# Head attention in halves of a block: maxima, their transfer and the products per 1024 queries

## The chip, the cores and the metric

The kernel runs on one core of a Trainium2 chip. The metric is the device time of one execution in microseconds (us); the kernel before stands at a median of 3103.95 us. The engines are named as in the profile: PE (matmuls) with PEld (its weight loads), DVE (vector engine), ACT (scalar engine), POOL (GpSimd), and SP, which computes nothing and issues DMAs.

## What is computed

A transformer block with a fast feed-forward layer ahead of it and one behind it. The change is in the attention of the layer between them alone. Its reference, cut to what matters:

```python
q = x @ Wq.T + bq; k = x @ Wk.T + bk; v = x @ Wv.T + bv      # x: 2 x 2048 x 256
qm = q.reshape(d_batch * NB_HEADS, q_len, d_head)            # 32 x 2048 x 16, and km, vm
att = softmax(einsum('nqd,nkd->nqk', qm, km), axis=-1)
...
att_out = einsum('nqk,nkd->nqd', att + batch_pos, vm)        # batch_pos: position bias by head
```

So there are 32 independent blocks (16 heads, 2 batches), each with 2048 queries and 2048 keys of 16 numbers.

## The kernel before

`head_attend` handles the 32 blocks one after another (`BLOCKS` = 32, `n` is the block, `n // 2` the head). A block's 2048 rows are 16 chunks of 128 (`RC` = 16) or four groups of 512 (`QG` = 4). Every engine runs its own program in a fixed order and meets the others by semaphores only. The work of a block:

- **Scans.** `scan(n, e)` on PE, 64 for a block: one chunk of 128 queries against 512 keys, into one of four PSUM banks (`s1_ps`). DVE takes the maximum of two banks at a time (`scan_max`, L1538), 32 for a block. A bank comes free when its maximum is done.
- **Maxima.** `max_parts` on DVE, four small instructions among the first four scan maxima of the next block: the maximum of each query over the four key groups (`nmax`, L1545), its two parts (`mparts`, L1549, L1552), and a transpose in 32 x 32 squares (`mT`, L1558). `load_m` on SP then issues 8 DMAs (L1281) that bring `mT` into two rows of the query stack `qs`, so that the score matmul subtracts the maximum by itself.
- **Scores.** `score(n, c, g)` on PE (L1456), 64 for a block: 128 keys on the partitions against 512 queries, into one of three PSUM turns; ACT takes the exponential into `probs` (L1603), 64 for a block.
- **Products.** `products` on PE (L1467) adds the values times `probs` in one PSUM bank, four matmuls a half, two chunks behind the scores (`LATE` = 2). When the last chunk is in, DVE transposes the bank and takes a reciprocal (`turn_out`, L1565, L1568), and POOL finishes and stores the block (`finish`).
- **Positions.** For each head two `positions` pieces on PE (L1483, 11 matmuls each) once POOL has prepared its sums; ACT copies them out (L1593) and SP stores them (`store_pos`, L1303).

`step(n)` on PE interleaves the scans of later blocks with the scores of block `n`: scan and score alternate, and after each second pair comes a half of products. At its start it waits for the maxima of its block (`m_loaded`). The scans lead by a whole block and 24 (`LEAD` = 6 chunks of 4): before `step(0)` PE has issued 88 scans and both position pieces of head 0, and after the last scan 88 scores are left.

SP's program for block `n`, in this order: wait until the last score of block `n - 1` is made; 12 loads of queries and keys for block `n + 2` (`load_qk`, L902); for even `n` up to 24 five loads for a later head (`load_head`: L1293, L1294, L1295, and two of L1297) and up to 22 one more DMA (`skew`, L1285); two stores of positions (`store_pos`); and last `load_m(n + 1)`. SP issues strictly in that order, and a wait holds everything behind it.

Of the kernel before, what the change touches and what calls it, by code (L numbers as in the profile page):

```python
# [1173 lines left out]
def head_attend(nc, tag, stacks, scan_loaded, ones_set, parts_d, v_d, table_d, skew_d, pos_d, att_d):  # L1174
# [3 lines left out]
    with ExitStack() as ctx:  # L1178
# [14 lines left out]
        UNIT = RC * QG  # L1193
        SCANS = RC * QG
        LEAD, LATE = 6, 2
# [11 lines left out]
        probs = sb("probs", [P, LATE + 1, ROWS])  # L1207
        mx = sb("mx", [P, SLOTS * SCANS])
        nmax = sb("nmax", [P, RC])
        mparts = sb("mparts", [P, PARTS, RC], F32R)  # L1210
        mT = sb("mT", [P, PARTS * RC])
# [32 lines left out]
        MLOADS = QUADS * PARTS  # L1244
# [8 lines left out]
        for n in range(BLOCKS):  # L1253
            for c in range(RC):
                for g in range(QG):
                    turn_of["score", n, QG * c + g] = len(turn_of)
                if c == POS_AT and n // 2 + 1 < HEADS:
                    turn_of["pos", n // 2 + 1, n % 2] = len(turn_of)

        def scores_done(n):  # L1260
            return turn_of["score", n, UNIT - 1] + 1
# [177 lines left out]
        def _(pe):  # L1439
            def scan(n, e):  # L1440
                count = SCANS * n + e
                if e % 2 == 0 and count >= BANKS:
                    pe.wait_ge(s1_free, (count - BANKS) // 2 + 1)
                c, g = e // QG, e % QG
                nc.tensor.matmul(s1_ps[:, e % BANKS, :], qs[0:QKROWS, n % SLOTS, c, :],  # L1445
                                 ks[0:QKROWS, n % SLOTS, g * 4:(g + 1) * 4, :].rearrange("p c t -> p (c t)"),
                                 start=True, stop=True).then_inc(s1_made, 1)
# [6 lines left out]
            def score(n, c, g):  # L1454
                out = take_turn(turn_of["score", n, QG * c + g])
                nc.tensor.matmul(out, ks[LOW:LOW + KR, n % SLOTS, c, :],  # L1456
                                 qs[LOW:LOW + KR, n % SLOTS, g * 4:(g + 1) * 4, :].rearrange("p c t -> p (c t)"),
                                 start=True, stop=True).then_inc(s2_made, 1)

            def products(n, c, half):  # L1460
                if half == 0:
                    pe.wait_ge(s2_free, turn_of["score", n, QG * c + QG - 1] + 1)
                elif c == 0:
                    return
                at, size = (0, 512) if c == 0 else (half * HALF, HALF)
                for g in range(QG):
                    last = nc.tensor.matmul(o_ps[g * COLS:(g + 1) * COLS, at:at + size], vs[:, n % SLOTS, c, :],  # L1467
                                            probs[:, (n + c) % (LATE + 1), g * 512 + at:g * 512 + at + size],
                                            start=(c == 0), stop=(c == RC - 1 and half == 1), tile_position=(0, g * COLS))
                if c == RC - 1 and half == 1:  # L1470
                    last.then_inc(o_made, 1)
# [21 lines left out]
            def step(n):  # L1493
                pe.wait_ge(score_loaded[n % SLOTS], 16 * LOADS * (n // SLOTS + 1))
                pe.wait_ge(m_loaded, 16 * MLOADS * (n + 1))
                pe.wait_ge(v_placed, n + 1)
                for c in range(RC):
                    ahead = n + 1 if c < RC - LEAD else n + 2
                    if c == RC - LEAD and ahead < BLOCKS:
                        pe.wait_ge(scan_loaded[ahead % SLOTS], 16 * LOADS * (ahead // SLOTS + 1))  # L1500
                    for k in range(QG):
                        if ahead < BLOCKS:
                            scan(ahead, (c + LEAD) % RC * QG + k)
                        score(n, c, k)
                        if k % 2 == 0:
                            continue
                        if c >= LATE:
                            if c == LATE and k == 1 and n > 0:
                                pe.wait_ge(turn_step, 2 * n - 1)
                            products(n, c - LATE, k // 2)  # L1510
                        elif n > 0:
                            products(n - 1, RC + c - LATE, k // 2)
                    if c == POS_AT and n // 2 + 1 < HEADS:
                        positions(n // 2 + 1, n % 2)

            pe.wait_ge(constants_set, 4)
            pe.wait_ge(scan_loaded[0], 16 * LOADS)
            for e in range(SCANS // 2):
                scan(0, e)
            for half in range(2):  # L1520
                positions(0, half)
            for e in range(SCANS // 2, SCANS):
                scan(0, e)
            pe.wait_ge(scan_loaded[1], 16 * LOADS)
            for e in range(LEAD * QG):
                scan(1, e)
            for n in range(BLOCKS):
                step(n)
            for c in range(RC - LATE, RC):
                for half in range(2):  # L1530
                    products(BLOCKS - 1, c, half)

        @block.vector
        def _(dve):
            def scan_max(n, e):
                dve.wait_ge(s1_made, SCANS * n + e + 2)
                at = n % SLOTS * SCANS + e
                nc.vector.reduce_max(mx[:, at:at + 2], s1_ps[:, e % BANKS:e % BANKS + 2, :], AX_X).then_inc(s1_free, 1)  # L1538

            def max_parts(m, i):  # L1540

                if i == 0:
                    dve.wait_ge(s1_free, SCANS // 2 * (m + 1))
                    at = m % SLOTS * SCANS
                    nc.vector.reduce_max(nmax[:, :], mx[:, at:at + SCANS].rearrange("p (c g) -> p c g", g=QG),  # L1545
                                         AX_X, negate=True).then_inc(max_step, 1)
                elif i == 1:
                    dve.wait_ge(max_step, MSTEPS * m + 1)
# [471 lines left out]
```

## Time and profile before

| | |
|---|---|
| median of 3 runs | 3103.95 us (3103.12 to 3110.8) |
| profiled execution | 3088.07 us, span 3086.3 us |
| head attention, first scan to last exponential | 826.9 to 2205 us |
| busy over the whole span | PE 92%, DVE 69%, ACT 58%, POOL 29% |
| mean granted PE clock | 0.956 |

Times in the trace count from the span's start. A row of the timeline that merges several instructions (x8) gives the first start and the time until the last end. In brackets stands how long the engine had been idle, and what ended that. An SPq row is a DMA's issue on SP; its landing is later.

### The profile page before, as it was taken

What the parts mean: (1) busy time and instruction counts of PE and PEld (TensorE: products, weight loads), DVE (VectorE), ACT (ScalarE), POOL (GpSimd) and SP (SyncE); (2) the same over time, 40 slices, a digit from 0 to 9 for tenths busy, and PEclk for the clock granted to TensorE, in tenths of its full rate; (3) what the DMA queues carried; (4) which work ended last, traced back from release to release, by engine and by line L of the source; (5) the groups of instructions that cost most, each with busy time, mean ns of one, the idle gap of its engine ahead of it and who ended that gap; (6) DMA issues with size and microseconds to landing.
All of it is one profiled execution on the core that took longest, in us unless ns stands there. A gap on an engine that the chain in (4) does not pass through costs nothing. (4 is left out here: it accounts for less than half of the span.)

```text
span 3086.3 us, 56464 instructions
## 1 busy us (share of the span) xinstructions
PE 2843.5 (92%) x20746; PEld 1731.7 (56%) x20746; DVE 2130.9 (69%) x3331; ACT 1796.6 (58%) x3503; POOL 908.5 (29%) x1482
## 2 busy tenths in 40 slices
PE   5788999998799999999999999999795688899999
PEld 2677888886543333333333333333253377688888
DVE  5445555455589999999999999998053454555544
ACT  3345343334248888888888888888543244444333
POOL 4552310001343333333333333311112554220000
PEclk8999999998779999999999999999897799999999
DMA  8795210105935554444555554442233589221010
GB/s 248 241 298 161 66 40 28 31 25 201 277 49 67 67 67 54 58 60 60 67 67 67 67 64 56 48 48 32 76 105 123 168 284 287 83 63 30 28 31 21
DMA packets 447482, 302.13 MB, mean 98 GB/s; under 512 B 170840, under 2 KB 421820, under 8 KB 447212
## 3 DMA queue, kind: packets, MB, share of 16 engines
q1 hardware_dynamic: 413292, 214.59, 35.4%
q0 software_dynamic: 33920, 83.93, 8.6%
q8 instruction: 170, 2.79, 0.4%
q14 instruction: 100, 0.82, 0.1%
HBM read 183.27 MB, written 118.78 MB: 98 GB/s over the span
## 5 line engine op out<-in xcount | busy, mean ns | idle before, releaser
L1538 DVE TENSOR_REDUCE mx_ha<-s_ps_ha 128x2 f32<-128x1024 f32 x1024 | 1243.5, 1222 | 57.3 <-PE s_ps_ha L1445 49.7
L1603 ACT ACTIVATE probs_ha<-s_ps_ha 128x512 f32<-128x512 f32 x2048 | 1108.8, 595 | 192.7 <-PE s_ps_ha L1456 58.8
L1445 PE MATMUL s_ps_ha<-ks_ha,qs_ha 48*128 48x512 f32 x2048 | 759.3, 454 | 14.0 <-POOL onesr_ha L1411 8.4
L1456 PE MATMUL s_ps_ha<-qs_ha,ks_ha 50*128 50x512 f32 x2048 | 749.6, 446 | 0.8 <-ACT probs_ha L1603 0.2
L1467 PE MATMUL o_ps_ha<-probs_ha,vs_ha 128*32 128x256 f32 (+1 forms) x7936 | 646.7, 398 | 0.9 <-DVE oT_ha L1565 0.9
L1445 PEld LDWEIGHTS s_ps_ha<-ks_ha,qs_ha 48*128 48x128 f32 x2048 | 312.7, 190 | 441.5 <-DVE mx_ha L1538 373.1
L870 ACT ACTIVATE probsT_a<-pT_ps_a 128x512 fp32r<-128x512 f32 x256 | 146.4, 597 | 423.0 <-PE pT_ps_a L744 409.2
L1467 PEld LDWEIGHTS o_ps_ha<-probs_ha,vs_ha 128*32 128x32 f32 x7936 | 156.5, 108 | 359.7 <-issue 186.1
L1456 PEld LDWEIGHTS s_ps_ha<-qs_ha,ks_ha 50*128 50x128 f32 x2048 | 304.9, 185 | 33.0 <-ACT probs_ha L1603 32.6
L699 POOL DMA_INDIRECT rows_a<-ys_d,slots x96 | 90.9, 947 | 627.1 <-PE turn_ps_a L721 576.1
L1395 POOL TENSOR_TENSOR onorm_ha<-oT_ha,rinv_ha 128x256 f32<-128x256 f32 x32 | 19.9, 623 | 837.4 <-DVE rinv_ha L1568 837.4
L787 DVE TENSOR_REDUCE nmax_a<-s_ps_a 128x1 f32<-128x2048 f32 x64 | 146.7, 2292 | 162.2 <-PE s_ps_a L733 161.1
L444 DVE COPY y_p<-y_ps_p 128x256 f32<-128x256 f32 x282 | 119.5, 424 | 188.6 <-PE y_ps_p L574 126.4
L248 POOL DMA_INDIRECT xs_d<-xn_p,row_of_p x192 | 186.6, 972 | 202.3 <-PE xT_ps_p L538 88.6
L476 ACT ACTIVATE h_p<-h_ps_p,wa_p 65x128 f32<-65x128 f32 x282 | 102.7, 364 | 182.8 <-PE h_ps_p L564 141.3
L733 PE MATMUL s_ps_a<-k0T_a,qT_a 128*128 128x512 f32 x768 | 201.0, 406 | 1.9 <-DVE qT_a L801 1.9
L564 PE MATMUL h_ps_p<-xsT_p,wa_p 128*65 128x128 f32 x1128 | 175.3, 278 | 26.2 <-issue 23.4
L733 PE MATMUL s_ps_a<-k1T,qT_a 128*128 128x512 f32 x768 | 190.4, 398 | 0.0
L574 PE MATMUL y_ps_p<-leaf_w_p,h_p 65*128 x564 | 173.8, 390 | 16.5 <-ACT h_p L476 10.2
L766 PE MATMUL o_ps_a<-v_a,probsT_a 128*128 128x512 f32 x512 | 188.8, 408 | 0.0
L766 PE MATMUL o_ps_a<-v,probsT_a 128*128 128x512 f32 x512 | 188.6, 408 | 0.0
L564 PEld LDWEIGHTS h_ps_p<-xsT_p,wa_p 128*65 128x65 f32 x1128 | 133.6, 139 | 75.1 <-issue 45.3
(212 smaller groups left out, 3950.9 us busy)
## 6 DMA issues: line engine op xcount, KB each, us to landing
xs_p<-xs_d SPq DMA_DIRECT2D x282, 128.0 KB
ys_d<-y_p SPq DMA_DIRECT2D x66, 512.0 KB
qs_ha<-parts_d SPq DMA_DIRECT2D x192, 128.0 KB, 6.1
ks_ha<-parts_d SPq DMA_DIRECT2D x192, 128.0 KB, 6.7
parts_d<-parts_hp POOLq DMA_DIRECT2D x32, 512.0 KB, 7.5
xs_d<-y_p SPq DMA_DIRECT2D x6, 1024.0 KB
leaf_w_p<-in_wa SPq DMA_DIRECT2D x4, 1048.0 KB
leaf_w_p<-in_wb SPq DMA_DIRECT2D x4, 1040.0 KB
```

What stands on the lines that cost most here:

```text
L248: pool.indirect_dma_start(xs_d[f], bass.IndirectOffsetOnAxis(row_of[:, f, t:t + 1], 0), xn[:, t, :], None).then_inc(scattered[f], 16)
L564: last = nc.tensor.matmul(h_ps[0:W1C, n % 2, 0:P], wa[:, n % WB, c * W1C:(c + 1) * W1C], xsT[:, n % 2, c, :], start=(c == 0), stop=(c == C ...
L574: nc.tensor.matmul(y_ps[:, n % 2, 0:D], h[:, n % 2], leaf_w[0:W1C, n // SEG % 2, bass.ds(at + LA, D)], start=True, stop=True).then_inc(y_m ...
L733: last = nc.tensor.matmul(s_ps[:, g, :], qT[:, i % 2, hq, c, :], kT[b][:, hk, c, g * 512:(g + 1) * 512], start=(c == 0 and n == 0), stop=( ...
L766: nc.tensor.matmul(o_ps[:, :], probsT[:, 0, g, k * P:(k + 1) * P], value.rearrange("p h d -> p (h d)"), start=first, stop=False)
L787: nc.vector.reduce_max(nmax[:, :], s_ps[:, :, :].rearrange("p a b -> p (a b)"), AX_X, negate=True).then_inc(max_done, 1)
L870: nc.scalar.activation(probsT[:, 0, g, :], pT_ps[:, g % 2, :], ACT.Identity).then_inc(pT_high, 1)
L1445: nc.tensor.matmul(s1_ps[:, e % BANKS, :], qs[0:QKROWS, n % SLOTS, c, :], ks[0:QKROWS, n % SLOTS, g * 4:(g + 1) * 4, :].rearrange("p c t - ...
L1456: nc.tensor.matmul(out, ks[LOW:LOW + KR, n % SLOTS, c, :], qs[LOW:LOW + KR, n % SLOTS, g * 4:(g + 1) * 4, :].rearrange("p c t -> p (c t)") ...
L1467: last = nc.tensor.matmul(o_ps[g * COLS:(g + 1) * COLS, at:at + size], vs[:, n % SLOTS, c, :], probs[:, (n + c) % (LATE + 1), g * 512 + at ...
L1538: nc.vector.reduce_max(mx[:, at:at + 2], s1_ps[:, e % BANKS:e % BANKS + 2, :], AX_X).then_inc(s1_free, 1)
L1603: nc.scalar.activation(probs[:, (n + c) % (LATE + 1), g * 512:(g + 1) * 512], s2_ps[:, turn % TURNS, :], ACT.Exp).then_inc(s2_free, 1)
```

## The change

A block becomes two units `u` (`UNITS` = 64), each with half of its queries, that is 1024 of them: chunks 0, 1, 4, 5, 8, 9, 12, 13 for the even unit, and the others for the odd one (`chunk_of`). A unit has 32 scans, 32 scores and 32 exponentials of the same sizes as before, and 16 chunks of products with four matmuls each. Everything that was done once a block with the maxima is done once a unit: the four small DVE instructions on 8 columns where there were 16, and `load_m`, which now has 16 DMAs of 4 rows where there were 8 of 16 rows. `mT` has two buffers. `LEAD` = 12 chunks of 2 is again 24 scans, but now beyond a unit: 56 scans come ahead of the first score, and 56 scores behind the last scan. The two position pieces of head 0 stand behind 40 and 48 scans, where both stood behind 32. The wait for the constants comes behind the first 32 scans.

The core of the diff:

```diff
-        UNIT = RC * QG
-        SCANS = RC * QG
-        LEAD, LATE = 6, 2
+        UNITS = 2 * BLOCKS
+        UC = RC // 2
+        PAIR = 2
+        UNIT = RC * PAIR
+        SCANS = UC * QG
+        RING = 2 * SLOTS
+        LEAD, LATE = 12, 2
...
-        MLOADS = QUADS * PARTS
+        MLOADS = QUADS * PARTS * 2
...
+        def chunk_of(u, e):
+
+            k = e // QG
+            return k % QUADS * QUADS + u % 2 * 2 + k // QUADS
...
-            def load_m(n):
-                sp.wait_ge(mT_made, n + 1)
+            def load_m(u):
+                k = u // 2 % SLOTS
+                sp.wait_ge(mT_made, u + 1)
                 for i in range(QUADS):
                     for part in range(PARTS):
                         row = LOW + QKROWS + part
-                        at = i * COLS + part * RC
-                        sp.dma_start(qs[row:row + 1, n % SLOTS, :, i * COLS:(i + 1) * COLS].bitcast(F32),
-                                     mT[at:at + RC, :]).then_inc(m_loaded, 16)
+                        for b in range(2):
+                            at = i * COLS + part * UC + b * QUADS
+                            chunks = qs[row:row + 1, k, u % 2 * 2 + b::QUADS, i * COLS:(i + 1) * COLS]
+                            sp.dma_start(chunks.bitcast(F32), mT[at:at + QUADS, u % 2, :]).then_inc(m_loaded, 16)
...
+            load_m(0)
             for half in range(2):
                 store_pos(0, half)
-            load_m(0)
             for n in range(BLOCKS):
...
                 if n // 2 + 1 < HEADS:
                     store_pos(n // 2 + 1, n % 2)
+                load_m(2 * n + 1)
                 if n + 1 < BLOCKS:
-                    load_m(n + 1)
+                    load_m(2 * n + 2)
...
-            def step(n):
-                pe.wait_ge(score_loaded[n % SLOTS], 16 * LOADS * (n // SLOTS + 1))
-                pe.wait_ge(m_loaded, 16 * MLOADS * (n + 1))
-                pe.wait_ge(v_placed, n + 1)
+            def step(u):
+                n = u // 2
+                if u % 2 == 0:
+                    pe.wait_ge(score_loaded[n % SLOTS], 16 * LOADS * (n // SLOTS + 1))
+                    pe.wait_ge(v_placed, n + 1)
+                pe.wait_ge(m_loaded, 16 * MLOADS * (u + 1))
...
+            for u in range(UNITS):
                 for e in range(0, SCANS, 2):
-                    scan_max(n, e)
-                    if n > 0 and e // 2 <= MSTEPS:
-                        max_parts(n - 1, e // 2)
+                    scan_max(u, e)
+                    if u > 0 and e // 2 <= MSTEPS:
+                        max_parts(u - 1, e // 2)
```

On SP, the program of one block with head loads (`n` = 0), behind the 12 loads of `load_qk`; `mT_made` is the semaphore of the transpose, `s2_free` that of the copied positions, `s2_made` that of the scores. Before:

```order
L1293 DMA band_ha<-skew_d 128x384
L1294 DMA far_ha<-skew_d 128x128
L1295 DMA far_ha<-skew_d 128x128
L1297 DMA vp_ha<-vh_d 128x16x16 x2
...
L1303 DMA pos_d<-pos_ha 128x8x16 [waits s2_free_ha]
L1303 DMA pos_d<-pos_ha 128x8x16
L1281 DMA qs_ha<-mT_ha 1x16x32 [waits mT_made_ha]
L1281 DMA qs_ha<-mT_ha 1x16x32 x7
L902 DMA qs_ha<-parts_d 16x16x128 [waits s2_made_ha]
```

The same place after the change:

```order
L1305 DMA band_ha<-skew_d 128x384
L1306 DMA far_ha<-skew_d 128x128
L1307 DMA far_ha<-skew_d 128x128
L1309 DMA vp_ha<-vh_d 128x16x16 x2
...
L1315 DMA pos_d<-pos_ha 128x8x16 [waits s2_free_ha]
L1315 DMA pos_d<-pos_ha 128x8x16
L1294 DMA qs_ha<-mT_ha 1x4x32 [waits mT_made_ha]
L1294 DMA qs_ha<-mT_ha 1x4x32 x15
L1294 DMA qs_ha<-mT_ha 1x4x32 [waits mT_made_ha]
L1294 DMA qs_ha<-mT_ha 1x4x32 x15
L902 DMA qs_ha<-parts_d 16x16x128 [waits s2_made_ha]
```

Behind the same loads and stores now stand 32 DMAs in two batches with a wait each: the first is for the second half of the block under way, the second for the first half of the next block.

On DVE, the maxima of the first block and what follows them, before:

```order
L1538 TENSOR_REDUCE mx_ha<-s_ps_ha 128x2 [waits s1_made_ha] x33
L1545 TENSOR_REDUCE nmax_ha<-mx_ha 128x16 [waits s1_free_ha]
...
L1558 STREAM_TRANSPOSE mT_ha<-mparts_ha 128x32 [waits max_step_ha]
L1538 TENSOR_REDUCE mx_ha<-s_ps_ha 128x2 [waits s1_made_ha] x29
L1545 TENSOR_REDUCE nmax_ha<-mx_ha 128x16 [waits s1_free_ha]
```

The same after the change:

```order
L1547 TENSOR_REDUCE mx_ha<-s_ps_ha 128x2 [waits s1_made_ha] x17
L1554 TENSOR_REDUCE nmax_ha<-mx_ha 128x8 [waits s1_free_ha]
...
L1567 STREAM_TRANSPOSE mT_ha<-mparts_ha 128x32 [waits max_step_ha]
L1547 TENSOR_REDUCE mx_ha<-s_ps_ha 128x2 [waits s1_made_ha] x13
L1554 TENSOR_REDUCE nmax_ha<-mx_ha 128x8 [waits s1_free_ha]
```

The first maxima come after 17 large reduces, where it was after 33, and from one transpose to the next unit's first small reduce stand 13 large ones where there were 29.

## Rows read from the trace of the kernel before

**Rows 1.** The page's costliest groups, for the head attention's DVE and ACT.

```profile
L1538 DVE TENSOR_REDUCE mx_ha<-s_ps_ha 128x2 f32<-128x1024 f32 x1024 | 1243.5, 1222 | 57.3 <-PE s_ps_ha L1445 49.7
L1603 ACT ACTIVATE probs_ha<-s_ps_ha 128x512 f32<-128x512 f32 x2048 | 1108.8, 595 | 192.7 <-PE s_ps_ha L1456 58.8
```

**Rows 2.** Windows in mid-attention: window, length, PE, PEld, DVE, ACT, POOL, clock, DMA.

```profile
1300.00:1600.00 300.00, 299.85 (x2816) 117.30 (x2818) 290.09 (x277) 254.66 (x474) 108.74 (x233) 1.00 0.54 66
```

**Rows 3.** Timeline of SP, a block with head loads and the next.

```profile
1466.28 0.33 SPq L902 DMA_DIRECT2D qs_ha<-parts_d  x1
...
1475.90 6.53 SPq L1297 DMA_DIRECT2D vp_ha<-vh_d  x2
...
1484.90 1.22 SPq L1303 DMA_DIRECT2D pos_d<-pos_ha  x2
1498.87 4.94 SPq L1281 DMA_DIRECT2D qs_ha<-mT_ha  x8
1507.39 0.33 SPq L902 DMA_DIRECT2D qs_ha<-parts_d  x1
...
1514.76 3.25 SPq L1303 DMA_DIRECT2D pos_d<-pos_ha  x2
```

**Rows 4.** Timeline of all engines where a step starts.

```profile
1499.97 13.56 DVE L1538 TENSOR_REDUCE mx_ha<-s_ps_ha 128x2 f32<-128x1024 f32 x11
...
1507.83 0.18 PEld L1445 LDWEIGHTS s_ps_ha<-ks_ha,qs_ha 48*128 48x128 f32 x1 [0.41 <-issue]
...
1508.17 0.39 PE L1445 MATMUL s_ps_ha<-ks_ha,qs_ha 48*128 48x512 f32 x1
```

**Rows 5.** Instructions on `mT`, `mparts` and `nmax`: ns min/median/max, first and last start.

```profile
L1281 SPq DMA_DIRECT2D qs_ha<-mT_ha x256: 502/589/1864, 881.0 to 2156.3; - x128
L1558 DVE STREAM_TRANSPOSE mT_ha<-mparts_ha x32: 194/200/211, 880.8 to 2151.7; 128x32 f32<-128x32 f32 x32
...
DMA to landing us min/median/max: 1.6/1.7/3.4
...
L1549 DVE CAST mparts_ha<-nmax_ha x32: 161/162/185, 877.6 to 2151.2; 128x16 fp32r<-128x16 f32 x32
L1552 DVE TENSOR_TENSOR mparts_ha<-nmax_ha,mparts_ha x32: 164/166/805, 878.9 to 2151.4; 128x16 fp32r<-128x16 f32 x32
...
L1545 DVE TENSOR_REDUCE nmax_ha<-mx_ha x32: 207/207/220, 876.4 to 2151.0; 128x16 f32<-128x64 f32 x32
```

**Rows 6.** Timeline of the head attention's first stretch.

```profile
826.92 2.07 PE L1445 MATMUL s_ps_ha<-ks_ha,qs_ha 48*128 48x512 f32 x4 [8.35 <-POOL onesr_ha L1411]
...
849.26 2.07 SPq L1297 DMA_DIRECT2D vp_ha<-vh_d  x2
...
850.59 2.29 PE L1483 MATMUL s_ps_ha<-vpp_ha,bandp_ha 128*128 128x256 f32 x9 [3.58 <-POOL distantp_ha L1356]
...
855.44 10.81 DVE L1538 TENSOR_REDUCE mx_ha<-s_ps_ha 128x2 f32<-128x1024 f32 x9 [7.17 <-PE s_ps_ha L1445]
...
889.81 0.79 PE L1456 MATMUL s_ps_ha<-qs_ha,ks_ha 50*128 50x512 f32 x1
```

**Rows 7.** The last scan in the timeline, and the exponentials of all blocks.

```profile
2149.30 0.39 PE L1445 MATMUL s_ps_ha<-ks_ha,qs_ha 48*128 48x512 f32 x1
...
L1603 ACT ACTIVATE probs_ha<-s_ps_ha x2048: 589/597/617, 890.6 to 2204.4; 128x512 f32<-128x512 f32 x187
```

**Rows 8.** Timeline of SP: a DMA of 128 rows (`wo`) and one of 3 rows (`bo`).

```profile
2221.63 0.42 SPq L1682 DMA_DIRECT2D wo_hc<-in_wo  x1
2222.10 0.35 SPq L1682 DMA_DIRECT2D bo_hc<-in_bo  x1
```

**Rows 9.** Windows, as in Rows 2, behind stretches in which PE did little.

```profile
890.00:900.00 10.00, 9.91 (x45) 5.66 (x46) 7.10 (x6) 5.99 (x12) 2.45 (x5) 0.61 1.23 121
...
2655.00:2660.00 5.00, 1.19 (x7) 1.19 (x8) 2.06 (x3) 2.65 (x4) 0.58 (x1) 0.92 0.09 26
2660.00:2665.00 5.00, 4.51 (x17) 3.31 (x15) 4.53 (x12) 4.74 (x15) 0.96 (x1) 0.74 0.02 3
```

More of the change, by code:

```diff
@@ L1452, in take_turn, with score, products @@
                 return s2_ps[:, turn % TURNS, :]
[L1454 to L1457, printed above, removed]
-                                 start=True, stop=True).then_inc(s2_made, 1)
[L1460 to L1470, printed above, removed]
+            def score(u, c, g):
+                out = take_turn(turn_of["score", u, PAIR * c + g])
+                k, first = u // 2 % SLOTS, u % 2 * 2
+                queries = qs[LOW:LOW + KR, k].rearrange("p (j c) t -> p j (c t)", c=QUADS)[
+                    :, 2 * g:2 * g + 2, first * P:(first + 2) * P]
+                nc.tensor.matmul(out.rearrange("p (j t) -> p j t", j=2), ks[LOW:LOW + KR, k, c, :], queries,
+                                 start=True, stop=True).then_inc(s2_made, 1)
+            def products(u, c):
+                pe.wait_ge(s2_free, turn_of["score", u, PAIR * c + PAIR - 1] + 1)
+                at = u % 2 * HALF
+                for i in range(QUADS):
+                    last = nc.tensor.matmul(o_ps[i * COLS:(i + 1) * COLS, at:at + HALF], vs[:, u // 2 % SLOTS, c, :],
+                                            probs[:, (RC * u + c) % (LATE + 1), i, :],
+                                            start=(c == 0), stop=(c == RC - 1), tile_position=(0, i * COLS))
+                if c == RC - 1 and u % 2 == 1:
                     last.then_inc(o_made, 1)
@@ L1491, in positions @@
                 add(onesr[:, :], distantp[:, k, 1], 0, stop=True).then_inc(s2_made, 1)
-            def step(n):
-                pe.wait_ge(score_loaded[n % SLOTS], 16 * LOADS * (n // SLOTS + 1))
-                pe.wait_ge(m_loaded, 16 * MLOADS * (n + 1))
-                pe.wait_ge(v_placed, n + 1)
-                for c in range(RC):
[L1498 to L1513, printed above, removed]
@@ new lines, in step @@
+            def step(u):
[4 more added lines that the diff above has]
+                pe.wait_ge(m_loaded, 16 * MLOADS * (u + 1))
+                for c in range(RC):
+                    ahead = PAIR * (c + LEAD)
+                    to, e = u + 1 + ahead // SCANS, ahead % SCANS
+                    if to % 2 == 0 and e == 0 and to < UNITS:
+                        pe.wait_ge(scan_loaded[to // 2 % SLOTS], 16 * LOADS * (to // 2 // SLOTS + 1))
+                    for k in range(PAIR):
+                        if to < UNITS:
+                            scan(to, e + k)
+                        score(u, c, k)
+                    if c >= LATE:
+                        if c == LATE and u % 2 == 0 and n > 0:
+                            pe.wait_ge(turn_step, 2 * n - 1)
+                        products(u, c - LATE)
+                    elif u > 0:
+                        products(u - 1, RC + c - LATE)
+                    if c == POS_AT and u % 2 == 0 and n // 2 + 1 < HEADS:
@@ L1514, in step @@
                         positions(n // 2 + 1, n % 2)
+            pe.wait_ge(scan_loaded[0], 16 * LOADS)
+            for e in range(SCANS):
+                scan(0, e)
             pe.wait_ge(constants_set, 4)
[L1517 to L1524, printed above, removed]
@@ L1525, in _ @@
-            for e in range(LEAD * QG):
+            for e in range(LEAD * PAIR):
+                if e % 8 == 0 and e > 0:
+                    positions(0, e // 8 - 1)
                 scan(1, e)
-            for n in range(BLOCKS):
-                step(n)
+            for u in range(UNITS):
+                step(u)
             for c in range(RC - LATE, RC):
-                for half in range(2):
-                    products(BLOCKS - 1, c, half)
+                products(UNITS - 1, c)
         @block.vector
```

92 lines of the change are left out of this document (48 added, 44 removed).

## The prediction

> **What bounds the kernel now.** I read the page's costliest groups first. DVE's large maximum and ACT's exponential are the two big groups of the head attention: 1024 of 1222 ns and 2048 of 595 ns [rows 1]. Then a window in its middle: DVE works 290.1 of 300 us, ACT 254.7, and PE is shown busy throughout, at a granted clock of 1.00 [rows 2]. A busy PE says little here, so I looked at the timeline where a step starts: eleven maxima follow each other in 13.56 us, 1.233 us each, while PE's next scan had stood idle 0.41 us [rows 4]. So PE waits for DVE, and the attention runs at DVE's pace: a block takes 1507.39 - 1466.28 = 41.11 us from one last score to the next [rows 3], of which 32 large maxima are 39.5 and the four small instructions 0.735 (207, 162, 166 and 200 ns) [rows 5].
>
> The third view is the queue of SP, which the change loads. After a block's last score SP issues loads and stores for 1486.12 - 1466.28 = 19.84 us in a block with head loads, and until 1518.01, that is 10.6 us, in one without [rows 3]. Then it sits until the maxima are transposed. From the first issue of `load_m` (1498.87) to PE's first scan in the new step (1507.83) there are 8.96 us [rows 3, 4]. The eight DMAs need 7 x 0.6175 us (4.94 / 8) and 1.7 us to land, 6.0 us [rows 3, 5]. So 3.0 us are spare, and nobody waits for the maxima today.
>
> **What the change removes.** Two things at the ends. (1) Behind the last scan (2149.3) the exponentials go on until 2205 [rows 7]: 88 scores at some 0.62 us. 56 are left afterwards, so 32 x 0.62 = 19.9 us fewer, where DVE stays the bound. (2) Ahead of the first position piece PE waits 3.58 us for POOL, and DVE then has been idle 7.17 us [rows 6]. Eight scans later POOL's sums (850.6) are just there; two idle spells of some 1 us remain, a gain of 5 us. That the first score comes at some 863 instead of 889.8 [rows 6] gives nothing by itself, as DVE has the same 1024 maxima to do.
>
> **What it adds on DVE.** The small instructions come 64 times, not 32. On half the columns they are nearly as long, since their shortest kin of 16 columns take 162 ns and the transpose keeps its shape [rows 5]. I take 0.70 us a unit (bounds 0.37, half of now, and 0.735), so 2 x 0.70 - 0.735 = 0.66 us more a block, 21 us in all. By (1), (2) and this the time would hardly move: -4 us.
>
> **What it adds on SP decides.** `load_m` has 16 DMAs for each unit. Its window does not grow: from a unit's transpose to the scan that opens the next step there are the same seven maxima, 8.96 us. The issue of a 4-row DMA is not in the trace. Upper bound: as now, 0.6175 us with the gap. Lower bound: the 3-row DMA at 0.35 us, 0.38 with the gap [rows 8]. That one reads from memory, while a 128-row neighbour of it takes 0.42, so few rows save 0.07 to 0.11 us of it; taken from 0.589 [rows 5], with the gap, this gives 0.51, my value. The last lands 15 x 0.51 + 1.7 = 9.35 us after the first issue, 9.45 with an allowance of 0.1 for waking PE. That is 0.5 us beyond the window.
>
> A page puts the landing otherwise: the Trainium skill, "DMA: Bandwidth & Descriptors", section "Anatomy of one DMA", gives a DMA a fixed cost of about 2.0 us, which doesn't shrink with its size. The trace shows 1.7 us for this very transfer [rows 5]; by the page's figure each unit would wait 0.3 us longer, an estimate of 19 us over 62 units. I go by the trace.
>
> Once the wait is in the loop, the unit's time is a cycle. From the scan that opens the step: 0.73 us until DVE has its two banks (1507.83 to 1508.56) [rows 4], 8 maxima of 1.233, small ones of 0.70, makes 11.3 us to the next transpose; then 9.45. That is 20.75 us for an odd unit. The even one also has the block's turn-out and positions: 41.11 - 39.46 - 0.735 = 0.9 us now, and I take 1.2, since DVE's slack to hide them is used up. A block without head loads: 2 x 20.75 + 1.2 = 42.7 us.
>
> In the 13 blocks with head loads (n = 0, 2, ..., 24) the order on SP costs more. `load_m(2n + 1)` stands behind 19.84 us of loads and stores, and these start with the last score of the unit before. The maxima are ready some 13 us after it and wait for the queue. They are in at 19.84 + 9.45 = 29.3 us; the even unit's step began at 0.8 (20.75 less 19.9 us of scores), so it lasts 28.5 us, and the block 28.5 + 20.75 = 49.25. Behind the waiting PE stand scans, scores and products alike, so DVE and ACT stop too. The long piece of SP's list is the two `vp` loads, 6.53 us [rows 3]; they are unchanged.
>
> Sum. The first step starts at 863: SP is free at 851.3, the first unit's maxima are transposed at some 853.5 (20 maxima of 1.233 behind 826.9, with 1.2 us for the first scans and 0.70), then 9.45 [rows 6]. 13 x 49.25 + 18 x 42.7 = 1409, with 1 more for block 0, whose four position stores now come behind its `load_m`: the last block starts at 2273. Its two units take 19.9 and 19.5 us of scores: the end is at 2312, against 2205, so **+107 us**; both ends' gains are in this.
>
> To that comes the clock. Behind a stretch in which PE did 1.19 us of work in 5, the granted clock is 0.74 over the next 5 us, about 2.6 us at the 1.2 GHz level; behind the opening scans it is 0.61 over 10 us, 7.8 us at that level [rows 9]. PE's work in 1.233 us is 0.83 (0.41 idle) [rows 4], 1.66 at half the clock: a quarter of that time is lost, 0.7 to 2.0 us. With a stop of some 7 us in each of 13 blocks: 9 to 26 us, I take 18. Together +125 us. The profiled execution has 3088.07 us, so 3213 there; it lies 16 us under the median of the runs, whose 3103.95 gives **3229 us**.
>
> **The rivals.**
> - *A 4-row DMA costs as much as one of 16 rows.* For it: that all eight take the same time [rows 3, 5]. Then 15 x 0.6175 + 1.8 = 11.06 us, a unit 22.36, a plain block 45.9, one with head loads 19.84 + 11.06 - 2.46 + 22.36 = 50.8. Sum 1487 from 864.5 on: +187, with the clock +205: 3309 us.
> - *It costs 0.38.* For it: the 3-row row [rows 8]; against: it is another kind of transfer. Then 7.5 us, inside the window. Plain blocks run at DVE's pace, 41.11 + 0.66 = 41.8; those with head loads take 19.84 + 7.5 - 0.4 + 20.4 = 47.3. Sum 1367 from 861 on: +64, with the clock +82: 3186 us.
> - *The clock falls at every unit.* PE stops at each step for the maxima. A gap of 0.41 us at each pair leaves 1.00 now [rows 2, 4], and mine of 0.8 is not much longer, which speaks against it. It would cost 0.7 to 2.0 us for 51 more units, +69: 3298 us. The Trainium skill, "TensorE: Matmul & The Clock Gate", section "HAM oscillation — how this bites in real kernels", describes this: PE stops for a DMA at every tile and starts each one throttled.
> - *The queue is through in time: not slower.* The price hangs on the `vp` pair: 6.53 us behind the loads, but 2.07 us when the queue is empty [rows 3, 6]. From the point at which SP is free some 13.4 us after the last score (20.9 - 7.5), with DMAs of 0.38, nothing waits. Then -4 us: 3100 us. Against it: the loads ahead of the pair stay. If the small instructions fell into DVE's idle 9.9 us in 300 [rows 2] as well: -25, 3079 us.
>
> **How the numbers follow.** Chances: my forecast 0.52 (its own range 3200 to 3265), full price 0.19, low price 0.15, clock at every unit 0.07, in time 0.05, and faster 0.02. The range runs from under the low price with no clock loss (3104 + 64 = 3168) to the full price with 26 us of it (3104 + 187 + 26 = 3317) and a little over: 3165 to 3325. It leaves the last two cases out, and some of the tails. Within 0.3% (9 us) is about what a measurement can't tell from no change. Faster 0.02, same 0.05, slower 0.93.
>
> **What the profile after would show.** Right: the issue of `qs_ha<-mT_ha` at some 0.48 us, x1024; in 13 blocks an SP timeline where these issues follow the position stores without a pause, and there a DVE wait for scans of 6 to 8 us; DVE busy for 0.84 of a block with head loads and 0.97 of a plain one; the first score near 863; the last exponential near 2312. Wrong: maxima at 97% in all blocks, an issue of 0.59 or 0.35, or `vp` loads of 2 us. The largest single doubt is the issue time of the small DMA: 0.1 us of it is worth 35 us downwards and 75 us upwards.

## The result and the profile after

| | before | after |
|---|---|---|
| median of 4 runs | 3104.83 us | 3546.56 us (3528.43 to 3568.62) |
| ratio | | 1.1424, 95% interval 1.1382 to 1.1467 |
| profiled execution | 3088.07 us | 3529.82 us, span 3528.0 us |
| head attention, first scan to last exponential | 1378 us | 835.3 to 2641.0, 1806 us |
| mean granted PE clock | 0.956 | 0.867 |

The change costs 442 us, not 125. Of it 428 lie in the head attention; the first scan also comes 8 us later, and that start varies between 810.5 and 835.3 in the profiles below without regard to the edits.

The costliest groups of the page after, in the place of [rows 1]; at the end of a row stands the idle time ahead of the group:

```profile
L1547 DVE TENSOR_REDUCE mx_ha<-s_ps_ha 128x2 f32<-128x1024 f32 x1024 | 1241.6, 1220 | 475.3 <-PE s_ps_ha L1458 472.0
L1614 ACT ACTIVATE probs_ha<-s_ps_ha 128x512 f32<-128x512 f32 x2048 | 1112.0, 595 | 586.9 <-PE s_ps_ha L1472 495.5
L1458 PE MATMUL s_ps_ha<-ks_ha,qs_ha 48*128 48x512 f32 x2048 | 887.0, 519 | 202.0 <-DMA qs_ha<-mT_ha 184.0
```

DVE and ACT do the same work at the same durations and now stand idle for 475 and 587 us, waiting for PE. PE itself waits 184 us for the maxima, which it didn't do before. 184 is far from 428: a second loss is in there. The windows show it, one of 300 us as in [rows 2] and six of 5 us around one stop:

```profile
1300.00:1600.00 300.00, 263.16 (x2117) 97.30 (x2115) 216.77 (x226) 187.74 (x348) 75.70 (x163) 0.81 0.37 45
1570.00:1575.00 5.00, 0.00 (x0) 0.00 (x0) 0.55 (x1) 0.21 (x1) 0.19 (x1) 0.74 0.01 1
1575.00:1580.00 5.00, 2.25 (x14) 0.79 (x14) 0.99 (x1) 1.09 (x2) 0.00 (x0) 0.50 0.00 0
1580.00:1585.00 5.00, 5.00 (x28) 1.81 (x28) 2.68 (x3) 2.17 (x4) 0.00 (x0) 0.50 0.00 0
1585.00:1590.00 5.00, 5.00 (x32) 1.60 (x32) 2.73 (x4) 2.75 (x6) 0.00 (x0) 0.50 0.00 0
1590.00:1595.00 5.00, 5.00 (x40) 1.61 (x36) 3.77 (x7) 2.99 (x7) 0.00 (x0) 0.71 0.00 0
1595.00:1600.00 5.00, 5.00 (x56) 1.82 (x48) 4.97 (x5) 4.42 (x9) 0.00 (x0) 1.00 0.02 4
```

PE stands still at 1570 and works without a gap from 1577.75 on, but at 0.50, the 1.2 GHz level, until about 1592. In mid-attention the mean granted clock is 0.81, where it was 1.00. Over the whole attention the clock records hold 44 stretches at the low level, 724 us together. The first of them, 61 us, lies behind the opening scans; before it was the only one, of 37.5 us. The other 43 come later, among the stops, 662 us together.

SP's timeline of that block, one with head loads, against [rows 3]:

```profile
1545.88 0.44 SPq L902 DMA_DIRECT2D qs_ha<-parts_d  x1
...
1553.35 9.69 SPq L1309 DMA_DIRECT2D vp_ha<-vh_d  x2
1563.08 2.14 SPq L1297 DMA_DIRECT2D skew_d<-table_d  x1
1565.26 1.21 SPq L1315 DMA_DIRECT2D pos_d<-pos_ha  x2
1566.52 38.31 SPq L1294 DMA_DIRECT2D qs_ha<-mT_ha  x32
```

The first of the 32 follows the position stores without a pause: the maxima had been waiting for the queue. What happens where they are in, in the timeline of all engines (compare [rows 4]; bracketed idle time and what ended it):

```profile
1577.75 0.79 PE L1458 MATMUL s_ps_ha<-ks_ha,qs_ha 48*128 48x512 f32 x1 [7.89 <-DMA qs_ha<-mT_ha]
...
1578.61 1.09 ACT L1614 ACTIVATE probs_ha<-s_ps_ha 128x512 f32<-128x512 f32 x2 [8.40 <-PE s_ps_ha L1472]
...
1578.90 1.08 PE L1479 MATMUL o_ps_ha<-probs_ha,vs_ha 128*32 128x256 f32 x8
1579.01 1.22 DVE L1547 TENSOR_REDUCE mx_ha<-s_ps_ha 128x2 f32<-128x1024 f32 x1 [8.46 <-PE s_ps_ha L1458]
1579.91 0.79 PE L1458 MATMUL s_ps_ha<-ks_ha,qs_ha 48*128 48x512 f32 x1
...
1582.07 0.79 PE L1458 MATMUL s_ps_ha<-ks_ha,qs_ha 48*128 48x512 f32 x1
...
1606.09 0.47 PE L1458 MATMUL s_ps_ha<-ks_ha,qs_ha 48*128 48x512 f32 x1 [2.04 <-DMA qs_ha<-mT_ha]
```

All three engines stop for some 8 us. Then PE starts its pairs 2.16 us apart (1577.75, 1579.91, 1582.07) instead of 1.233, and DVE waits in every one of them. The next unit, which has no head loads ahead of it, waits too: 2.04 us. The transfer itself, in the list of the instructions on `mT` (compare [rows 5]):

```profile
L1294 SPq DMA_DIRECT2D qs_ha<-mT_ha x1024: 572/573/1283, 862.3 to 2617.2; - x171
L1567 DVE STREAM_TRANSPOSE mT_ha<-mparts_ha x64: 192/200/211, 862.1 to 2607.7; 128x32 f32<-128x32 f32 x64
...
  PE s_ps_ha L1458: 184.0, 50
```

A 4-row DMA takes 573 ns, and one issue starts 0.616 us after the one before it (median). From the first issue to the scan that waits for all sixteen it is thus 15 x 0.616 + 1.6 = 10.9 us, against the 8.96 us that the next seven maxima give. The last line says that PE waits for this transfer 50 times, 184.0 us in all. From one block's first load to the next's, blocks with head loads take 54.7 to 65.7 us, mean 60.8, the plain ones some 52; before, it was 41.1 from the second block on.

### The profile page after: what moved, and what is told of

Its sections match the earlier page's. It is cut to its first block and busy times, and to the rows that moved or that the text cites. A ratio compares the mean times of both kernels' runs of the same rounds, so it can differ in the third digit from the quotient of the medians.

```text
span 3528.0 us, 57937 instructions
## 1 busy us (share of the span) xinstructions
PE 3091.0 (88%) x21002; PEld 1801.9 (51%) x21002; DVE 2152.0 (61%) x3460; ACT 1798.9 (51%) x3503; POOL 909.2 (26%) x1482
## 5 line engine op out<-in xcount | busy, mean ns | idle before, releaser
L1458 PE MATMUL s_ps_ha<-ks_ha,qs_ha 48*128 48x512 f32 x2048 | 887.0, 519 | 202.0 <-DMA qs_ha<-mT_ha 184.0
L1472 PE MATMUL s_ps_ha<-qs_ha,ks_ha 50*128 50x512 f32 x2048 | 875.4, 512 | 0.0
L1479 PE MATMUL o_ps_ha<-probs_ha,vs_ha 128*32 128x256 f32 x8192 | 774.8, 456 | 0.7 <-DVE oT_ha L1575 0.7
L1458 PEld LDWEIGHTS s_ps_ha<-ks_ha,qs_ha 48*128 48x128 f32 x2048 | 360.4, 219 | 729.6 <-issue 324.5
L1479 PEld LDWEIGHTS o_ps_ha<-probs_ha,vs_ha 128*32 128x32 f32 x8192 | 172.6, 116 | 450.5 <-ACT probs_ha L1614 241.5
L1472 PEld LDWEIGHTS s_ps_ha<-qs_ha,ks_ha 50*128 50x128 f32 x2048 | 353.7, 215 | 11.5 <-ACT probs_ha L1614 11.1
```

The costliest lines, as they stand in the source:

```text
L1458: nc.tensor.matmul(s1_ps[:, e % BANKS, :], qs[0:QKROWS, k, c, :], ks[0:QKROWS, k, g * 4:(g + 1) * 4, :].rearrange("p c t -> p (c t)"), sta ...
L1472: nc.tensor.matmul(out.rearrange("p (j t) -> p j t", j=2), ks[LOW:LOW + KR, k, c, :], queries, start=True, stop=True).then_inc(s2_made, 1)
L1479: last = nc.tensor.matmul(o_ps[i * COLS:(i + 1) * COLS, at:at + HALF], vs[:, u // 2 % SLOTS, c, :], probs[:, (RC * u + c) % (LATE + 1), i, :],
```

## The experiments

Two suspects, then, that feed each other: the transfer of the maxima (too many DMAs, and too late in SP's order) and the granted clock behind each stop. All ratios are to the kernel before on the same chip, whose median was 3067 to 3068 us for `e1` to `e8` and 3100.76 for `e9`, `e10`, `x1` and `x2`.

| run | ratio (95%) | blocks, us | at 1.2 GHz, us |
|---|---|---|---|
| after | 1.1424 (1.1382 to 1.1467) | 52 / 61 | 724 |
| `e1_m_before_heads` | 1.1174 (1.1102 to 1.1247) | 46 to 61, mean 52.5 | 707 |
| `e2_filler` | 1.1055 (1.1001 to 1.1108) | 45.5 / 54 to 66 | 341 |
| `e3_before_16_loads` | 1.0706 (1.0682 to 1.0729) | 46.7 to 50.7 | 341 |
| `e4_8_loads` | 1.1287 (1.1268 to 1.1306) | 54.1 | 55 |
| `e5_8_merged` | 1.0349 (1.0317 to 1.0380) | 41.2 / 53 | 273 |
| `e6_8_merged_order` | 0.9932 (0.9916 to 0.9949) | 41.2 | 65 |
| `e7_filler_both` | 1.0734 (1.0701 to 1.0766) | 45.6 / 53 | 68 |
| `e8_early_maxima` | 1.1092 (1.1053 to 1.1132) | 44 to 66 | 679 |
| `x1_half_products` | 0.9958 (0.9945 to 0.9972) | 40.7 | 41 |
| `x2_more_small_dve` | 0.9997 (0.9984 to 1.0011) | 41.1 | 41 |
| `e9_early_first` | 0.9956 (0.9936 to 0.9976) | 41.3 | 75 |
| `e10_lead9` | 1.0039 (1.0025 to 1.0054) | 41.6, one 52.0, one 46.0 | 99 |

Blocks are given as plain / with head loads where these differ. The last column adds the stretches of the clock records that lie in or reach into the time from the first score to the last exponential; 40 to 75 us of it is the one stretch behind the opening, which every run has.

**The order on SP: `e1_m_before_heads`.** The kernel after, with the odd unit's transfer ahead of the head loads:

```diff
+                if n // 2 + 1 < HEADS:
+                    store_pos(n // 2 + 1, n % 2)
+                load_m(2 * n + 1)
                 if n % 2 == 0 and n // 2 + SLOTS < HEADS:
                     load_head(n // 2 + SLOTS)
...
-                if n // 2 + 1 < HEADS:
-                    store_pos(n // 2 + 1, n % 2)
-                load_m(2 * n + 1)
```

> The changed kernel, but SP issues store_pos and load_m(2n+1) ahead of the head loads instead of behind them. Theory N (16 DMAs of 0.605 us for each unit outlast their window, so PE stops at every unit and its clock falls; the queue order only adds to it in 13 blocks): the blocks with head loads, 60.7 us on average in the changed kernel, become like the plain ones (52.3 us), 13 x 8.4 = 109 us less: 3435 us. Theory Q (the queue order is the cause of nearly everything): the gain comes back, 3110 to 3150 us.

It gave 78 us back (0.025 of 3104.83). The two kinds of block became alike, and PE's wait for the maxima fell from 184 to 111 us; but those 111 are still 50 waits of some 2 us, and the time at 1.2 GHz hardly fell. The order costs something, and is not the main thing.

**The stops without the clock, first try: `e2_filler`.** The kernel after, but ahead of its wait for the maxima PE repeats the next scan, so that it never stands still: 8 times, or 32 in front of a unit that waits behind head loads. The real scan overwrites the bank.

```diff
+                    for i in range(FILL if u % 2 == 0 or n % 2 or n > 24 else FILL_LONG):
+                        nc.tensor.matmul(s1_ps[:, e % BANKS, :], ...)
                 pe.wait_ge(m_loaded, 16 * MLOADS * (u + 1))
```

> The changed kernel, but ahead of each wait for the maxima PE repeats the next scan's matmul into its own free bank: 8 times (1.7 us at 2.4 GHz), and 32 times (6.8 us) where the head loads stand ahead in the queue. Nothing else waits for less. Theory C (more than half of the loss is the lower clock behind each stop, not the stop): the granted clock stays near 1.00, blocks take 46 and 51 us, the total is 3291 us. Rival (the stops are the loss and the low clock is hidden behind DVE and ACT): the clock rises and the time stays, 3520 to 3560 us.

The plain blocks came out at 45.5 us, as expected; those with head loads didn't. One of their stops, in PE's timeline and in windows:

```profile
1514.50 8.63 PE L1515 MATMUL s_ps_ha<-ks_ha,qs_ha 48*128 48x512 f32 x32
1524.43 0.79 PE L1459 MATMUL s_ps_ha<-ks_ha,qs_ha 48*128 48x512 f32 x1 [1.30 <-DMA qs_ha<-mT_ha]
```
```profile
1515.00:1520.00 5.00, 5.00 (x23) 4.04 (x23) 0.26 (x1) 0.00 (x0) 1.00 (x1) 1.00 0.08 9
1520.00:1525.00 5.00, 3.70 (x12) 2.40 (x12) 0.00 (x0) 0.00 (x0) 0.00 (x0) 0.57 0.01 1
1525.00:1530.00 5.00, 5.00 (x32) 1.49 (x32) 2.45 (x2) 2.55 (x5) 0.00 (x0) 0.50 0.00 0
```

PE was busy with fillers through 1515 to 1523, and yet the granted clock was 0.57 over 1520 to 1525. These fillers use rows 0 to 47 of the array alone.

**Second try: `e7_filler_both`.** Scan and score repeated in turn, that is rows 0 to 47 and rows 64 to 111, 7 or 36 pairs.

> As e2_filler, but the filler alternates the scan's matmul (rows 0 to 47) with one on rows 64 to 111, as steady work does: 7 pairs ahead of each wait, 36 where the head loads stand ahead. In e2 the clock fell while 32 fillers on rows 0 to 47 alone were running. Theory C: now it stays at 1.00, the blocks with head loads take 51 instead of 58.5 us: ratio 1.074 against 1.1055 in e2, 3334 us. Rival (the low clock there is harmless): 1.10 or more.

```profile
1300.00:1600.00 300.00, 292.83 (x2761) 129.23 (x2759) 245.42 (x256) 213.42 (x396) 90.65 (x195) 1.00 0.43 54
```

Now the clock holds, 1.00 over the 300 us, with one low stretch of 13.7 us behind the opening's. The order and the 16 DMAs are those of the kernel after, and the repeats hardly delay the scan: it starts 1.68 us after the transfer's last issue began (median), where it is 1.63 (odd units) and 1.83 (even ones) in the kernel after, when PE waits for the transfer. So this run divides the loss: 0.0734, that is 228 us, is what the stops cost by themselves, and the other 214 us are what the clock costs behind them.

**The 16 DMAs without the halves: `e3_before_16_loads`.** The kernel before, with each of its 8 DMAs cut in two of 8 rows:

```diff
-                        at = i * COLS + part * RC
-                        sp.dma_start(qs[row:row + 1, n % SLOTS, :, i * COLS:(i + 1) * COLS].bitcast(F32),
-                                     mT[at:at + RC, :]).then_inc(m_loaded, 16)
+                        for b in range(2):
+                            at = i * COLS + part * RC + b * RC // 2
+                            sp.dma_start(qs[row:row + 1, n % SLOTS, b * RC // 2:(b + 1) * RC // 2, ...
```

> The kernel before, with each of the 8 DMAs of load_m split into two of 8 rows: 16 DMAs for a block, nothing halved otherwise. Theory N: 15 x 0.605 + 1.7 = 10.8 us against a window of 8.96, so PE stops some 1.9 us once in a block and the clock falls behind it as in the changed kernel's plain units: 32 x (1.5 + 3.2) = +150 us, 3255 us (3150 if the clock holds). Theory Q and theory H (the halving itself costs: more small DVE work, other products) expect no change, 3104 us.

It costs 0.0706 with nothing halved. DVE's timeline from the transpose of the maxima (1453.50) on:

```profile
1453.63 9.83 DVE L1540 TENSOR_REDUCE mx_ha<-s_ps_ha 128x2 f32<-128x1024 f32 x8
1466.93 1.23 DVE L1540 TENSOR_REDUCE mx_ha<-s_ps_ha 128x2 f32<-128x1024 f32 x1 [3.48 <-PE s_ps_ha L1447]
1469.15 1.22 DVE L1540 TENSOR_REDUCE mx_ha<-s_ps_ha 128x2 f32<-128x1024 f32 x1 [0.99 <-PE s_ps_ha L1447]
1471.32 1.23 DVE L1540 TENSOR_REDUCE mx_ha<-s_ps_ha 128x2 f32<-128x1024 f32 x1 [0.94 <-PE s_ps_ha L1447]
```

A wait of 3.48 us, then waits of some 0.95 at each maximum, as PE is slow: a stop of a few us and its clock cost 5.6 to 9.6 us a block. It came out dearer than expected: the 8-row DMA takes 632 ns, so that one issue starts 0.676 us after another and not 0.605, and the rest is put down to the clock, which this run doesn't divide from the stop.

**Eight DMAs, by other halves: `e4_8_loads`.** A unit is eight neighbouring chunks, so that 8 DMAs of 8 rows do; each exponential then lies in one 512-query group, and the products are two matmuls of 512 columns instead of four of 256.

```diff
-            return k % QUADS * QUADS + u % 2 * 2 + k // QUADS
+            return u % 2 * UC + k
...
-                for i in range(QUADS):
-                    last = nc.tensor.matmul(o_ps[i * COLS:(i + 1) * COLS, at:at + HALF], ...
+                for g in range(PAIR):
+                    i = u % 2 * PAIR + g
+                    last = nc.tensor.matmul(o_ps[i * COLS:(i + 1) * COLS, :], ...
```

> The changed kernel with a unit of 8 neighbouring chunks instead of every other pair, so that load_m needs 8 DMAs of 8 rows for each unit instead of 16 of 4; products are 2 matmuls of 512 columns instead of 4 of 256; the queue order stays. Theory N: the maxima are in within the window, plain blocks take DVE's pace of 41.8 us; those with head loads still stop once (19.84 + 4.94 + 1.2 us after the last score, 5 us late, and some 5 us of low clock): 51 us. Together 3104 + 114 = 3218 us. Theory H: still above 3500 us.

A miss: no low stretch behind the opening's and no wait for a DMA, and yet every block takes 54.1 us. PE's timeline tells why:

```profile
1500.44 0.39 PE L1457 MATMUL s_ps_ha<-ks_ha,qs_ha 48*128 48x512 f32 x1
...
1500.77 1.05 PE L1477 MATMUL o_ps_ha<-probs_ha,vs_ha 128*32 128x512 f32 x4
1501.75 0.50 PE L1457 MATMUL s_ps_ha<-ks_ha,qs_ha 48*128 48x512 f32 x1
```

The products take 0.98 us to the next scan (1500.77 to 1501.75). In the kernel after, at the same clock, eight of 256 columns take 0.57. The columns are as many, but they go to two groups of 32 array columns instead of four. The group grows from 1.233 to 1.65 us and PE is the bound. The edit had changed two things, the products and the DMAs, so it couldn't speak for the transfer.

**Eight DMAs, the halves kept: `e5_8_merged`, and with the order of the first run: `e6_8_merged_order`.** Both parts of the maximum are laid side by side in `mparts`, and one DMA of 8 rows fills both rows of `qs`; halves, products and scores are those of the kernel after.

```diff
-                    for part in range(PARTS):
-                        row = LOW + QKROWS + part
-                        for b in range(2):
-                            at = i * COLS + part * UC + b * QUADS
-                            chunks = qs[row:row + 1, k, u % 2 * 2 + b::QUADS, i * COLS:(i + 1) * COLS]
-                            sp.dma_start(chunks.bitcast(F32), mT[at:at + QUADS, u % 2, :]).then_inc(m_loaded, 16)
+                    for b in range(2):
+                        at = i * COLS + b * PARTS * QUADS
+                        chunks = qs[row:row + PARTS, k, u % 2 * 2 + b::QUADS, i * COLS:(i + 1) * COLS]
+                        sp.dma_start(chunks.bitcast(F32), mT[at:at + PARTS * QUADS, u % 2, :]).then_inc(m_loaded, 16)
```

> The changed kernel (same halves, scans, products and queue order), with the parts of the maxima laid out so that one DMA fills both rows of qs: 8 DMAs of 8 rows for each unit instead of 16 of 4. Theory N (issues outlast the window, clock falls behind each stop): 7 x 0.65 + 1.7 = 6.3 us fit into 8.96, plain blocks take 41.8 us, those with head loads still stop for some 6 us and then run at low clock: 53 us. Ratio to before 1.045, 3244 us. Theory H (the halving itself costs): it stays above 1.10.

> Both cures in one: 8 merged DMAs for each unit, and load_m(2n+1) ahead of the head loads. Theory N and Q together explain all: every block takes DVE's pace of 41.8 us, the granted clock is 1.00 throughout, and what is left is the change's own balance, 21 us of small DVE instructions against 25 us at the two ends: ratio 0.998, 3097 us (3085 to 3110). If the halving costs something of its own, the ratio is 1.02 or more.

With 8 DMAs alone the plain blocks are back at 41.2 us, while those with head loads stay at 48 to 60. With the order as well, all are at 41.2, and the kernel is 0.7% faster than before:

```profile
1300.00:1600.00 300.00, 298.45 (x2885) 115.59 (x2881) 294.63 (x309) 256.13 (x474) 106.07 (x227) 1.00 0.48 60
```
```profile
1528.95 4.33 SPq L1314 DMA_DIRECT2D pos_d<-pos_ha  x2
1534.44 5.39 SPq L1293 DMA_DIRECT2D qs_ha<-mT_ha  x8
1539.87 0.40 SPq L1304 DMA_DIRECT2D band_ha<-skew_d  x1
...
1541.26 2.00 SPq L1308 DMA_DIRECT2D vp_ha<-vh_d  x2
```

The transfer stands ahead of the head loads and is through in 5.39 us (603 ns each); the `vp` pair takes 2.00 us there, not 9.69. Neither edit did it alone: the order left 0.1174, the eight DMAs left 0.0349, both together -0.0068.

**The maxima earlier: `e8_early_maxima`.** The four small DVE instructions stand right behind the next unit's first maximum instead of among the first four; otherwise the kernel after.

```diff
-                    if u > 0 and e // 2 <= MSTEPS:
-                        max_parts(u - 1, e // 2)
+                    if u > 0 and e == 0:
+                        for i in range(MSTEPS + 1):
+                            max_parts(u - 1, i)
```

> The changed kernel with its 16 DMAs for each unit, but the four small DVE instructions follow each other behind the first maximum of the next unit instead of one behind each of the first four: the transpose is 3.7 us earlier, the window 12.6 us less 0.2. Theory N (what counts is issue time against window): 15 x 0.605 + 1.7 = 10.8 us fit, plain blocks take 42.1 us, those with head loads still 60: ratio 1.076, 3339 us. Rival (16 DMAs cost something wherever they are, by the rings or the landing): above 1.10.

A miss. SP's timeline in a plain block, with DVE's transpose and PE's wait from the same stretch:

```profile
1591.79 0.45 SPq L902 DMA_DIRECT2D ks_ha<-parts_d  x1
1592.28 5.16 SPq L1315 DMA_DIRECT2D pos_d<-pos_ha  x2
...
1595.17 0.21 DVE L1567 STREAM_TRANSPOSE mT_ha<-mparts_ha 128x32 f32<-128x32 f32 x1
...
1597.49 11.13 SPq L1294 DMA_DIRECT2D qs_ha<-mT_ha  x16
...
1609.68 0.50 PE L1458 MATMUL s_ps_ha<-ks_ha,qs_ha 48*128 48x512 f32 x1 [2.00 <-DMA qs_ha<-mT_ha]
```

The maxima are transposed at 1595.38, but SP isn't free: the position stores stand ahead and hold it until 1597.44, 2.06 us longer. The 16 issues then take 11.13 us, where they take 9.8 with nothing just ahead of them, and PE waits 2.00 us. In this unit the place in the queue makes the stop. The whole trace says the same: the even units, whose transfer has nothing ahead of it, no longer stop at all, and 26 of the 31 odd units still do.

**Earlier, and first in the queue: `e9_early_first`.** The edit of `e8_early_maxima`, and `load_m(2 * n + 1)` ahead of head loads and position stores. All 16 DMAs stay.

> The changed kernel with its 16 DMAs of 4 rows for each unit, the four small DVE instructions right behind the next unit's first maximum (as in e8), and load_m(2n+1) ahead of the head loads and the position stores. Theory N and Q: the window is 12.4 us, SP is free when the maxima are made, 10.8 us fit: blocks at 41.2 us, clock 1.00, ratio 0.993 to 0.998. If 32 DMAs in a block cost something of their own, it is 1.01 or more.

0.9956: the 16 DMAs do no harm once they start early enough and nothing stands ahead of them. Blocks take 41.3 us at a granted clock of 1.00.

**All together with a shorter lead: `e10_lead9`.** Merged DMAs, early maxima, `load_m` first, and `LEAD` = 9, so that 50 scans come ahead of the first score.

> Everything that helped in one kernel: 8 merged DMAs for each unit, the maxima early, load_m(2n+1) first, and LEAD = 9 instead of 12, which leaves 50 scores behind the last scan instead of 56: 6 x 0.62 = 3.7 us less than e6 (ratio 0.9932), so 0.992. If the shorter lead brings stops back, above 1.00.

A miss. Blocks take 41.6 us instead of 41.3, one took 52.0 and one 46.0. In each of these two a small DVE instruction took 1.8 to 2.1 us instead of 0.17, and PE waited for the maxima behind it to free a bank. The one in the long block:

```profile
1395.11 2.11 DVE L1557 CAST mparts_ha<-nmax_ha 128x8 fp32r<-128x8 f32 x1
...
1398.82 0.50 PE L1457 MATMUL s_ps_ha<-ks_ha,qs_ha 48*128 48x512 f32 x1 [2.06 <-DVE mx_ha L1546]
```

Behind it the clock was low for 20.5 us, and 2.06 + 0.43 x 20.5 = 10.9 us is about what the block lost. Why the instruction took so long isn't shown. Nor is it shown what the shorter lead does, which wasn't tried by itself, and where the 0.3 us in each other block come from.

**What sets 1.233 us: `x1_half_products` and `x2_more_small_dve`.** Both are the kernel before with one engine's load changed: PE without half of the products behind the first chunk, and DVE with three more reduces of 0.207 us a block.

```diff
-                for g in range(QG):
+                for g in range(QG if c == 0 else QG // 2):
```
```diff
+                    for k in range(3):
+                        nc.vector.reduce_max(spare[:, m % 2, k], ...)
```

> The kernel before without half of its products: behind the first chunk only the groups 0 and 1 are added, so the attention output is incomplete. Theory P (the pace of 1.233 us for two scans, two scores and a product step is PE's own): PE's group shrinks by some 0.2 us and DVE sets the pace, 1.19 us a maximum; a block takes 39.7 instead of 41.1 us, the ratio is 0.986. Theory D (DVE sets the pace already): blocks stay at 41.1 us, ratio 1.000. If the granted clock falls with the lighter PE work, the run tells nothing.

> The kernel before with three more small reduces of 0.207 us a block on DVE, into a spare tile that nothing reads: 0.62 us a block, as much as the change adds. Theory P: DVE catches up, because its maxima can follow each other 1.19 us apart; a block takes 41.1 to 41.2 us, ratio 1.000 to 1.001. Theory D: 31 x 0.62 = 19 us more, ratio 1.006.

With half of the products gone a block takes 40.7 us, between the two expectations (39.7 and 41.1); with 0.62 us more on DVE it takes 41.1, the same. So DVE has room for that work. PE relieved gains only 0.4 us, as DVE's maxima, 1.22 us each, then follow each other without a gap: the two paces are 1.233 and 1.22 us.

## Why the prediction was wrong

**Right.** Direction, and both places: the transfer outlasts its window at nearly every unit (50 waits), and in the 13 blocks with head loads it waits in SP's queue (1565.26 to 1566.52 without a pause; DVE's wait there 8.46 us against 6 to 8 forecast). The four small instructions take 0.18, 0.16, 0.16 and 0.20 us (medians), the 0.70 I had taken. The first score is 41.0 us behind the first scan (835.3 to 876.3), where I had 36 (826.9 to 863).

The forecast was 107 us for stops less the ends' gains, and 18 for the clock. Measured are 228 and 214.

**The step that failed: the clock.** "PE's work in 1.233 us is 0.83 (0.41 idle), 1.66 at half the clock: a quarter of that time is lost, 0.7 to 2.0 us", once in each of 13 blocks, 18 us in all. The 0.41 was a PEld row: the weight loads' idle time, while the matmuls ran on. The row [rows 2] beside it, PE busy 299.85 of 300, said so, and so do PE's own rows at that place in the kernel before, where the scan starts while the last product is under way:

```profile
1507.26 0.64 PE L1467 MATMUL o_ps_ha<-probs_ha,vs_ha 128*32 128x256 f32 x8
1507.83 0.50 PE L1445 MATMUL s_ps_ha<-ks_ha,qs_ha 48*128 48x512 f32 x1
```

At 1.2 GHz the group takes 2.16 us: at least 0.93 of the 1.233 are array work, and 43% of each such stretch is lost. Second, I took the length of a low stretch from two windows [rows 9], 2.6 and 7.8 us; here those behind the opening last from 3.4 to 48 us, 15 on average. Third, I had them in 13 places, and there are 43. `e7_filler_both` against the kernel after gives the size, 214 us instead of 18. The trace of the kernel after leads to nearly the same sum by another way. PE works for 598 us of the 662 in those 43 stretches, and 0.43 of that are 257 us, an estimate; with the 184 us of waits they make 441. That the waits are fewer than the 228 us of `e7_filler_both` fits the slow PE giving the next transfer more time: at 11 of the 63 steps that open with a scan, the maxima are in before PE comes to it.

The rival "the clock falls at every unit" named this and had 7%. I held against it that a gap of 0.41 leaves the clock at 1.00, which is the same misread row. The Trainium skill, "TensorE: Matmul & The Clock Gate", section "HAM oscillation — how this bites in real kernels", describes PE stopping for a DMA at every tile and starting each one throttled; the windows from 1570 on agree with it (PE at nothing, then 0.50).

**A term of the wrong size: the issue.** I took 0.51 us with the gap, between 0.38 and 0.6175; it is 0.616, the upper bound, and the 0.573 without the gap is near the 0.59 that I had named as a sign of being wrong. The 3-row DMA of [rows 8] reads from memory and was no kin: few rows save next to nothing on a transfer out of `mT` (573 ns for 4 rows, 632 for 8, 589 for 16). With it the stops alone are those of the rival "a 4-row DMA costs as much as one of 16 rows": it had 45.9 and 50.8 us for the blocks and +187; `e7_filler_both`, at the full clock, has 45.6 and 53, and +228. Of the 41 us between, some 30 are the blocks with head loads, 2.2 us and more each.

**The two rivals came together.** Full price and clock were each priced against my forecast, so the range ended at 3325. A longer stop and a lower clock have one cause, and the first made the second likelier. By my own prices they would have given 187 + 18 + 69, some 3378 us; the rest is the clock's price.

**The landing.** 1.7 us a transfer was right: the last of 16 issues began at about 1576.1 (1566.52 + 10.18 - 0.57), and the scan at 1577.75 had it 1.6 us later. The 2.0 us that the Trainium skill, "DMA: Bandwidth & Descriptors", section "Anatomy of one DMA", gives is its figure for DMAs that GpSimd issues, which I had left out; these are issued on SP, and 2.0 would be too much here.

**Small terms.** 0.66 us a block for DVE's extra instructions: in `e6_8_merged_order` a block takes 41.2 us against 41.1, so it is 0.1, and `x2_more_small_dve` shows that DVE takes on 0.62 us more without a loss. "The attention runs at DVE's pace" was half of the truth, PE being as near to its bound. The ends: I had -25 us; the attention of `e6_8_merged_order` is 1365.3 us long (812.9 to 2178.2), 13 less than before, 16 with the 3 us of its blocks taken out.

So the halves are no loss by themselves. The change loses by the 16 DMAs in a window made for 8, by their place on SP, and by the clock that PE's stops cost.

## What to carry to other kernels

Where a change shortens the time between two uses of a small transfer, count its DMAs at the issue time that the same transfer has now, whatever their size, and compare the sum with the window before anything else. When PE is to wait anew and regularly, price the clock with the wait, by the ratio of its group at both levels (here 2.16 to 1.233 us), and read PE's own row for it, not that of the weight loads. Then look for the fewest DMAs and the first place in the queue together: here either alone left the kernel 3 to 12% slower, and both made it 0.7% faster than before.

## What the runs showed of the hardware

- Keeping PE busy didn't by itself keep the clock. While PE repeated 32 matmuls on rows 0 to 47 (1514.50 to 1523.13 in `e2_filler`) the granted clock fell: it was 1.00 over 1515 to 1520 and 0.57 over 1520 to 1525. With repeats in turn on rows 0 to 47 and 64 to 111 (`e7_filler_both`) it was 1.00 over 300 us.
- A DMA of the same 32-element rows costs SP 573 ns with 4 rows, 632 with 8, 589 with 16, and 603 with 8 rows into two partitions: all within some 10%. One issue starts 0.62 to 0.68 us after another.
- Four products of 32 x 512 columns on two column groups took 0.98 us to the next scan (`e4_8_loads`), eight of 32 x 256 on four groups 0.57 (kernel after), both at a granted clock of 1.00.
- The pair of `vp` loads took 9.69 us on SP right behind 15 other loads, and 2.00 behind the 8 small DMAs and three loads.
